# Layer 0 scores in two row halves of PE: three products of 16 rows per head, side jobs one to a unit

## What is computed

```python
xn = _layernorm(x)
qs = (xn @ Wq.T).reshape(b, s, 8, 2, 16)      # ks_ the same with Wk
vs = (xn @ Wv.T).reshape(b, s, 8, 32)
scores = einsum('bqhif,bkhif->ibhqk', qs, ks_) * 16 ** -0.5
atts = softmax(scores, axis=-1)
att = atts[0] - diff_weight * atts[1]
o = einsum('bhqk,bkhe->bqhe', att, vs)
s = ((o * rms(o) * norm_w).reshape(b, s, e) @ Wo.T + bo) * (1 - diff_weight)
g = silu(top-2-gated low-rank product of xn)   # _L0_ffn_ref
x = x + s * g
```

## Time and profile before

| | us |
|---|---|
| median of 3 runs (1444.07 to 1446.02) | 1444.89 |
| the profiled execution | 1444.3 |
| its span, first to last instruction | 1442.5 |
| PE busy | 1333.1 (92%) |
| DVE busy | 994.4 (69%) |
| ACT busy | 684.9 (47%) |
| POOL busy | 260.3 (18%) |
| layer 0's exponent products, first to last start | 55.2 to 759.3 |

### The profile page before, as it was taken

The page is one execution under the profiler, slowest core; times in us unless marked ns, Lnnn a source line. Parts: engine busy times, 40 slices in busy tenths (PEclk is TensorE's granted clock), DMA queues, the critical chain, the costliest instruction groups (busy, mean ns, idle before and its releaser), DMA issues. The chain is left out here.

```text
span 1442.5 us, 31653 instructions
## 1 busy us (share of the span) xinstructions
PE 1333.1 (92%) x11488; PEld 881.3 (61%) x11488; DVE 994.4 (69%) x2248; ACT 684.9 (47%) x1233; POOL 260.3 (18%) x330
## 2 busy tenths in 40 slices
PE   2899999999999999999996889999898989999997
PEld 2444455554555545555444768777776868687875
DVE  4666767767677676776646586868678686968675
ACT  3255655545555455554553344434444344444442
POOL 3000101011010110101012221313232231313131
PEclk8699999999999999999998799999999999999999
DMA  4746256362663626635207001001010101010000
GB/s 112 123 62 121 48 114 111 74 109 47 112 112 70 110 47 112 112 70 96 48 14 243 30 3 45 2 9 38 2 45 2 45 2 45 2 45 3 30 3 16
DMA packets 63483, 87.78 MB, mean 61 GB/s; under 512 B 8200, under 2 KB 37128, under 8 KB 63112
## 3 DMA queue, kind: packets, MB, share of 16 engines
q1 hardware_dynamic: 63376, 86.21, 29.6%
HBM read 58.92 MB, written 25.17 MB: 58 GB/s over the span
## 5 line engine op out<-in xcount | busy, mean ns | idle before, releaser
L799 DVE TENSOR_REDUCE negmax<-s_bank 128x1 f32<-128x512 f32 x512 | 331.4, 684 | 122.7 <-PE s_bank L533 122.6
L661 ACT ACTIVATE room<-t_bank 128x512 f32<-128x512 f32 x512 | 284.2, 597 | 157.5 <-PE t_bank L542 153.9
L542 PE MATMUL t_bank<-qst,kst 104*128 104x512 f32 x512 | 237.7, 466 | 9.3 <-ACT room L661 6.6
L533 PE MATMUL s_bank<-kst,qst 96*128 96x512 f32 x512 | 209.5, 416 | 14.6 <-DMA kst<-park 10.1
L542 PEld LDWEIGHTS t_bank<-qst,kst 104*128 104x128 f32 x512 | 96.8, 189 | 122.4 <-issue 79.8
L555 PE MATMUL a_bank<-room,v 128*32 128x512 f32 x1024 | 136.3, 604 | 0.0
L566 PE MATMUL d_bank<-room,pick 128*32 128x512 f32 x1024 | 133.3, 592 | 0.0
L533 PEld LDWEIGHTS s_bank<-kst,qst 96*128 96x128 f32 x512 | 100.2, 196 | 35.4 <-DVE negmax L799 11.9
L1542 DVE STREAM_TRANSPOSE pt<-ex 32x256 f32<-32x256 f32 x256 | 111.0, 433 | 10.1 <-POOL ex L1675 4.1
L1228 PE MATMUL pr<-xt_h,win_h 128*128 128x512 f32 x256 | 105.6, 413 | 0.0
L1228 PE MATMUL pr<-xt_h,win_l 128*128 128x512 f32 x256 | 100.1, 391 | 0.0
(11 more groups left out here) (254 smaller groups left out, 2322.0 us busy)
## 6 DMA issues: line engine op xcount, KB each, us to landing
qst<-park SPq DMA_DIRECT2D x128, 128.0 KB, 5.0
kst<-park SPq DMA_DIRECT2D x128, 128.0 KB, 5.6
park<-qk_h SPq DMA_DIRECT2D x32, 256.0 KB, 2.0
park<-qk_l SPq DMA_DIRECT2D x32, 256.0 KB, 2.0
room<-in_x SPq DMA_DIRECT2D x8, 512.0 KB, 4.8
xr<-in_x SPq DMA_DIRECT2D x8, 512.0 KB, 5.1
xb<-x SPq DMA_DIRECT2D x8, 512.0 KB, 4.4
xr<-x SPq DMA_DIRECT2D x8, 512.0 KB, 3.8
```

Of the source, the lines that this page charges most:

```text
L533: pe.matmul(s_bank[S_BANK[w]][:, :], qst[slot][0:MROW, j, c * P:(c + 1) * P], kst[slot][0:MROW, j, :], start=True, stop=True).then_inc(m.s ...
L542: pe.matmul(t_bank[w % 2][:, :], kst[slot][0:MROW + MROWS, j, c * P:(c + 1) * P], qst[slot][0:MROW + MROWS, j, :], start=True, stop=True). ...
L661: act.activation(probs[:, c, j, :], t_bank[w % 2][:, :], ACT.Exp, scale=SCALE0).then_inc(m.exp_done, 1)
L799: dve.tensor_reduce(negmax[:, i_par, c, j:j + 1], s_bank[S_BANK[w]][:, :], X, ALU.max, negate=True).then_inc(m.max_done, 1)
```

## The change

- `STACK` holds 3 products (the low x low one is dropped): 48 rows. Two heads stand side by side: the even head of a pair in rows 0 to 47, the odd one in rows 64 to 111, each with its two maximum rows (48, 49 and 112, 113) against rows of ones. A maximum product reads 48 partitions, an exponent product 50.
- Unit order: the exponent product of unit w takes row half w % 2, the maximum product issued right behind it takes the other half (`max_unit`). `LEAD` is 28.
- `park` takes five DMAs a half, `fill_stacks` four. Job M is one transpose of the 16 maximum columns; ACT and DVE take high and low parts, two DMAs place them.
- The zero rows and the `which` pattern go. POOL sets four stacks to 1.0 at the start.
- Side jobs stand behind even units, one each; `value_step` at w % 4 == 3, `denominators` one step later, at w % 4 == 1. So 58 of 64 units of a batch have a job behind them.
- ACT normalises x, copies `v` and `lc`, and scales `at` by -diff_weight; POOL adds the maps for all four tiles at once (`add_maps`) and forms `z` (`gated`). The squares on ACT wait for POOL's sum. DVE keeps one instruction of these in TA.
- The stores of x1 move behind M of half 2 on SP.

```diff
-STACK = 4 * F0
-MROW = 96
-MROWS = 2 * HG
-LEAD = 24
+PRODUCTS = 3
+STACK = PRODUCTS * F0
+ROWS = 64
+MROWS = 2
+LEAD = 28
...
+SLOTS = ((0, 0), (0, 2), (0, 4), (0, 6), (0, 8), (0, 10), (0, 12), (0, 14),
+         (1, 0), (1, 2), (1, 4), (1, 6), (1, 8), (1, 10), (1, 12), (1, 14),
+         (2, 0), (2, 2), (2, 4), (2, 6), (2, 8), (2, 10), (2, 12), (2, 14),
+         (3, 0), (3, 6))
+JOBS = (("PROJ", 3, 0), ("V", 0, 2), ("V", 0, 3), ("M", 1, 1), ("XT", 1, 0), ("XT", 1, 1), ("TD", -1, 0), ("TA", -1, 0),
+        ("PROJ", 4, 0), ("TA", -1, 1), ("TA", -1, 2), ("M", 2, 0), ("TA", -1, 3), ("V", 1, 0), ("OT", -1, 0), ("OT", -1, 1),
+        ("PROJ", 5, 0), ("ZT", -1, 0), ("WF", -1, 0), ("M", 3, 1), ("WF", -1, 1), ("WF", -1, 2), ("WF", -1, 3), ("V", 1, 1),
+        ("PROJ", 6, 0), ("M", 4, 0))
...
+GATE, GATE_EXP, GATE_END = (0, 13), (1, 1), (1, 5)
+SQUARES = ((1, 11), (1, 12), (1, 13), (1, 14))
+def max_unit(w):
+    return w // 8, w % 8 // 2, 1 - w % 2
...
             def fill_stacks(i, slot):
-                for r in range(4):
-                    for side, stack, part in ((0, qst, r // 2), (1, kst, r % 2)):
+                for odd in range(2):
+                    for side, stack in ((0, qst), (1, kst)):
...
                 if kind == "M":
-                    pe.wait_ge(m.m_low, i + 1)
-                    for c in range(QT):
-                        mm = pe.matmul(bank[MROW:MROW + MROWS, c * P:(c + 1) * P],
...
+                    pe.wait_ge(m.max_done, UNITS * (i + 1))
+                    pe.transpose(bank[0:HG * QT, 0:P], negmax[:, k, :, :].rearrange("p h c -> p (h c)"),
+                                 ident[:, :]).then_inc(m.m_psum, 1)
...
             def score_max(n, w, slot, i):
-                j, c = w // 4, w % 4
-                pe.matmul(s_bank[S_BANK[w]][:, :], qst[slot][0:MROW, j, c * P:(c + 1) * P], kst[slot][0:MROW, j, :],
+                j, c, odd = max_unit(w)
+                rows = slice(ROWS * odd, ROWS * odd + STACK)
+                pe.matmul(s_bank[S_BANK[w]][:, :], qst[slot][rows, j, c * P:(c + 1) * P], kst[slot][rows, j, :],
                           start=True, stop=True).then_inc(m.s_done, 1)
...
             def score_exp(g, w, slot, i):
-                c, j = w // 4, w % 4
+                c, j, odd = w // 4, w % 4 // 2, w % 2
+                rows = slice(ROWS * odd, ROWS * odd + STACK + MROWS)
+                pe.matmul(t_bank[w % 2][:, :], kst[slot][rows, j, c * P:(c + 1) * P], qst[slot][rows, j, :],
+                          start=True, stop=True).then_inc(m.t_done, 1)
...
                             if step >= 0:
                                 value_step(b, step // 4, step % 4)
+                        if w % 4 == 1:
+                            step = 4 * hf + w // 4 - LAG - 1
+                            if step >= 0:
                                 denominators(b, step // 4, step % 4)
...
                 if kind == "SQ":
-                    act.wait_ge(m.o_ok, QT * i + k + 1)
+                    act.wait_ge(m.o_ok, i + 1)
...
+            def normalise(b, tiles):
+                act.wait_ge(m.nmr_ok, b + 1)
+                wait(act, m.xt_psum, KC * b)
+                for t in tiles:
+                    act.activation(xn[:, t, :], xb[:, t, :], ACT.Identity, scale=rstd[:, t:t + 1],
+                                   bias=nmr[:, t:t + 1]).then_inc(m.xn_ok, 1)
...
+            def add_maps(b):
+                pool.wait_ge(m.an_ok, QT * (b + 1))
+                wait(pool, m.ot_psum, KC * b)
+                wait(pool, m.ss_ok, QT * b)
+                maps = an[:, :, :, :, :].rearrange("p t (g i) h e -> p t g i (h e)", g=2)
+                pool.tensor_tensor(o[:, :, :].rearrange("p t (g n) -> p t g n", g=2), maps[:, :, :, 0, :],
+                                   maps[:, :, :, 1, :], ALU.add).then_inc(m.o_ok, 1)
```

More of the change, by code:

```diff
@@ L248, in layer0 @@
         qk_h, qk_l = sb("qk_h", [P, S], F32R), sb("qk_l", [P, S], F32R)
-        qst = [sb(f"qst{i}", [P, HG, S], F32R) for i in range(HALF)]
-        kst = [sb(f"kst{i}", [P, HG, S], F32R) for i in range(HALF)]
+        qst = [sb(f"qst{i}", [P, HG // 2, S], F32R) for i in range(HALF)]
+        kst = [sb(f"kst{i}", [P, HG // 2, S], F32R) for i in range(HALF)]
         vnew = sb("vnew", [P, QT, WCAT])
@@ L405, in load_x @@
+            def place_max(i, slot):
+                rows = [qst[slot][STACK + a:P:ROWS, :, :].rearrange("o i q -> o (i q)").bitcast(F32) for a in range(MROWS)]
+                sp.wait_ge(m.m_high, i + 1)
+                sp.dma_start(rows[0], mh[:, :].bitcast(F32)).then_inc(m.m_placed, 16)
+                sp.wait_ge(m.m_low, i + 1)
+                sp.dma_start(rows[1], ml[:, :].bitcast(F32)).then_inc(m.m_placed, 16)
             def load_x(b):
@@ L437, in body @@
                         place_max(i, k)
[L438 to L441, removed]
+                        if hf == 2 and not (isinstance(b, int) and b < 1):
+                            for t in range(QT):
+                                store_x1(b - 1, t)
             def slots(b):
@@ L634, in _ @@
             over_batches(pe, body, 2)
-            for step in range(16 - LAG, 16):
-                value_step(B - 1, step // 4, step % 4)
+            for step in range(15 - LAG, 16):
+                if step >= 16 - LAG:
+                    value_step(B - 1, step // 4, step % 4)
                 denominators(B - 1, step // 4, step % 4)
@@ L737, in body @@
                                 side(kind, i, k)
-                        if not first and hf == 1 and w in (3, 5, 7, 9):
-                            side("SQ", b - 1, (w - 3) // 2)
+                        if not first and (hf, w) in SQUARES:
+                            side("SQ", b - 1, SQUARES.index((hf, w)))
             over_batches(act, body, 2)
-            act.wait_ge(m.a_done, 16 * B)
-            act.activation(at[:, 3, :], a_bank[:, :], ACT.Copy).then_inc(m.a_evac, 1)
+            values_out(HALF * B - 1, HALF - 1)
             side("DEV", B - 1, 0)
@@ L746, in _ @@
                 side(kind, i, k, last_banks[n % len(last_banks)])
-                if kind == "TA":
-                    side("SQ", i, k)
+                if (kind, k) == ("TA", QT - 1):
+                    for t in range(QT):
+                        side("SQ", i, t)
         @block.vector
@@ L929, in body @@
                             max_tile(HALF * UNITS * b + ahead, ahead % UNITS, ahead // UNITS % 2)
-                        if w == 7 and not (last and hf == 3):
-                            side("MS", HALF * b + hf + 1, (hf + 1) % 2)
                         if not last:
@@ L994, in residual @@
                 pool.tensor_tensor(x1_tile(b, k), xr[:, k, :], g_[:, k, :], ALU.add).then_inc(m.x1_ok, 1)
+            for slot in range(HALF):
+                pool.memset(kst[slot][:, :, :].bitcast(F32), 1.0).then_inc(m.ones, 1)
             pool.wait_ge(m.mhalf_ok, 1)
@@ L998, in _ @@
             rstd_of(0)
[L999 to L1006 removed]
+            add_parts(0)
             def body(b):
@@ L1763, in layout0 @@
         "pick": pick,
-        "which": which.reshape(MROWS, HG, S),
     }
```

224 lines of the change are left out of this document (93 added, 131 removed), and 6 rows, old and new, of tables (JOBS, SLOTS).

## The result

The changed kernel takes **1612.7 us** (median of 4, 1610.5 to 1613.1), against 1444.5 of the kernel before on the same chip: a ratio of 1.116 (1.114 to 1.118). The prediction was 1403 us with a range to 1456. It is wrong by sign and by 210 us.

A forecast was written before the change was run, and what follows sets the result against it. PE was taken as the bound, busy 87.99 of 90.2 us a batch. Eight batches at 5.2 us less gave 42 us off 1444.3, other parts 0: 1402, put at 1403 us for the median, range 1365 to 1456.

The forecast's parts named there:

- The other parts: Work outside PE's products (DVE, ACT, POOL, stalls, SP, start, end): put at 0 in all, with bounds.
- Start: PE's wait of 10.11 us for the stacks: 3 us gained by smaller stacks, less 2.4 for four more lead units.
- PE's block: Exponent and maximum product between jobs of another shape: 0.53 us with leaving, load and entering, 58 times a batch.
- Start of the pair: Exponent and maximum product in separate row halves start about 10 ns apart, their weight loads side by side.
- Rival 1: A block's second weight load waits for its first: 0.10 to 0.11 us more a block, 1449 us; chance 0.15.
- rival 2: The row halves of PE don't overlap: each block 0.23 us longer, 1510 us; chance 0.10.
- Rival 3: PE pays no drain between row-half products and the 26 full-height side jobs: 37 us less, 1366 us; chance 0.08.
- Rival 4: ACT's squares and then PE wait for POOL's addition of the maps: 1430 us; chance 0.13.
- The batch: One steady batch of layer 0, between copies of `v`: 85 us instead of 90.2, by 5.2 us less PE work.
- the stalls: PE's waits at side jobs: about 1 us gained against 1 us new a batch; 0, bounds -1 and +1.5.
- DVE's relief at 0: Taking some 6 of 62 us a batch off DVE gains nothing, because DVE is not the bound.
- The sum: Eight batches at 5.2 us less PE work each: 42 us off the whole time.

The follow-up runs named there:

- e1: The changed kernel with its parking DMAs cut into 12 a half, each with 32 rows as slowest dimension: 1405.7 us.
- e4: The kernel before with only its two parking DMAs a half given a target whose slowest dimension is 2: 1741.6 us.
- e2: The changed kernel with `park` laid out so parking writes 64 or 128 rows as slowest dimension, while the fillings read with 3: 1504.3 us.
- e7: e2 with stack rows ordered feature by product, so the fillings have 16 as slowest dimension: 1399.2 us.
- e3: The changed kernel with its slow parking kept, but the placing of the maxima moved ahead of the stacks' filling in SP's program: 1507.5 us.
- e5: e1 with both products of a unit in the same row half, so they cannot overlap: 1469.0 us.
- e9: The kernel before with only the normalisation of x moved from DVE to ACT, with two small POOL instructions it needs: 1448.4 us.
- e10: e7 with the normalisation one unit earlier and the gate's twelve small instructions moved to the last quarter of the batch: 1429.7 us.
- e6: e1 with the denominators directly behind the values, taking away 16 of the 58 blocks of a batch: 1458.4 us.

## Why the prediction was wrong

**The step that failed** is one sentence of "The other parts": SP "issues 9 instead of 10 DMAs a half", put at 0. It counted the DMAs and took no duration from issue to landing for the five new ones. The parking, 2.7 us before, became 16.3 us. The same omission stands under "Start", where 3 us were put for stacks that shrink. The maximum products waited 20.17 us there after 10.11, and the first of them started at 42.98 instead of 34.30. The prediction's sentence on what waits behind SP named stores and the next parking, and left out `place_max`, which stands behind `fill_stacks` and which PE needs every few units. A landing time would have made the order of SP's queue a question by itself: in 16 us PE comes through 12 units of 1.33 us. e1 shows the term's size, 207 us; e4, that it needs nothing else of the change; e2 and e7, that it is the slowest dimension on either side, not the number of DMAs or bytes; e3, that half of it comes through the order in SP's program.

With that term taken out, the rest can be compared with e1 and e7:

- *PE's block.* Predicted 0.53 us. In e1: 0.43 from the pair to the next job, and 0.10 to 0.12 for leaving it (the last product of a projection takes 0.33, from 374.67 to 375.00, against a pitch of 0.23; `d_bank` 1.00 against the 0.88 of `a_bank` in the earlier trace rows). 0.53 to 0.55. Right.
- *Start of the pair.* Predicted some 10 ns apart; it is 0.00 in the rows shown for e1 (0.12 once in the kernel after, at 412.21, behind a long wait). Rival 1 (weight loads in series, 0.11) and rival 2 (no overlap, 0.24) fall. e5 shows that rival 2 would have given 1469 us instead of 1510; a part of the difference is waits of PE that the prediction did not have on its account.
- *Rival 3, no drain against full-height jobs.* It falls: a projection behind a pair starts 0.43 after it, the same as the 32-column job, and the pair behind a projection 0.33 instead of 0.23. So the rule that the prediction weighed (the Trainium skill, TensorEngine Tiling, Key Properties) agrees with the trace for products in a row half beside full-height ones too.
- *Rival 4, waits for POOL's sum.* In 200 to 600 us of e1 no wait of PE for POOL is listed. Only at the end, with nothing to cover it, `t_bank` waits 3.8 us for `o`, and before it waited 4.3 for DVE's. The rival falls, and the end cost nothing where +1 was put: from the last exponent product to the first output product it is 19.5 us before (759.3 to 778.8) and 19.1 in e1 (720.0 to 739.1).
- *The batch.* Predicted 85.0 us, from 90.2. Measured 86.6 in e1 ((578.74 - 145.62) / 5) and 85.7 in e7 ((570.52 - 141.82) / 5). Over these five batches PE is busy for 88.0 us before, 82.8 in e1 and 82.7 in e7: 5.2 and 5.4 less, where 5.2 were predicted. Its idle time is 2.2 us before, 3.8 in e1 and 3.1 in e7: +1.6 and +0.9, where 0 was put with bounds of -1 and +1.5. So the term of PE's work was right, and the one of the stalls too small, at the bound or just over it in e1. The largest two waits are a projection for the emptying of `misc` (1.0 us a batch), which the prediction had named by kind, and `XT` for ACT's normalisation (1.2), which it had not: it priced that move as load on ACT, hidden behind PE.
- *DVE's relief at 0.* In a steady batch it is right, by e9; in the first one the move of the normalisation cost the kernel before 3 us, which no term foresaw. DVE is busy for 56.9 us, ACT for 52.1 and POOL for 14.5 in the batch of e1, against 56, 52 and 16.
- *The sum.* 42 us were expected from PE's work. Against the kernel before on the same chip e1 gains 40 and e7 46. The steady batches give less than foreseen (e1: 3.6 each, 18 for five), and the ends, which the prediction left at the same gain, more: up to the second copy of `v` it is 152.0 us before and 145.6 in e1, and from the seventh of the eight copies to the last exponent product 156.3 (602.97 to 759.3) and 141.3 (578.74 to 720.0). That the two errors nearly cancel is luck.

So a prediction of 1403 us was near to what the arithmetic of PE brings (1399 and 1406), and missed what the changed kernel is. The range to 1456 had no rival for a DMA at all. None of the four asked about the one kind of operation whose shape the change altered without a row to price it.

The 12 DMAs of e1 take longer than the 5 of e7 (6.8 and 4.6 us of parking) through their issue: 5.5 us (306.29 to 311.80) against 2.8 (300.37 to 303.21), with 1.3 and 1.8 us from there to the filling. Open stays why e5 costs 2 us a batch less of PE's time than its rows give, and what decides the fall of the clock.

## What to carry to other kernels

Price every new DMA from issue to landing, by the size of the slowest dimension on both of its sides: one that is 2 or 3 left most of the DMA engines idle, and laying out both sides so that 16, 64 or 128 rows come first, as in e7, cost nothing here. Then ask what stands behind the wait for it in the queue of the engine that issues it; a small DMA behind a long wait can be what the bound engine needs. Issuing it earlier helps only in part, if it then still lands behind the slow one (e3). When the bound engine is PE, a short wait can cost more than its length, since the granted clock may fall behind it, and jobs that look like a loss (a block between two side jobs) can be what covers a bank's emptying.

## What the runs showed of the hardware

- The rate of a DMA by its slowest dimension: at 2 a DMA share of 0.13 to 0.14 and 44 to 55 GB/s (after, e4), at 3 a share of 0.19 and 77 GB/s (e2), at 4 together with 2 a share of 0.26 and 56 GB/s in the first window behind the issue (after, 389 to 392), with 16 rows or more up to 184 to 197 GB/s (e7 and e2).
- An 8 KB DMA issued behind narrow parking DMAs was of use only when they had landed: in e3 PE could start 8.8 us after its issue (449.70 to 458.45), and so it was in all ten places where PE waited for it there, with 8.5 to 10.5 us.
- 48- or 50-row products of 512 columns in the two row halves of PE start 0.00 us apart, and the pair takes 0.43 until the next job, where two in one half take 0.67.
- The granted clock fell to 0.50 behind a wait of PE of 1.62 us in e10 and to 0.51 behind one of 0.89 us in e6, and stood at 1.00 through waits of up to 1.3 us in e7. What decides it was not tried.
